# Turning x and h by DMA instead of on TensorE in an attention and fp4 feed-forward kernel, with u's statistics on ScalarE

## The chip, the cores and the metric

The kernel runs on one core of a Trainium2 chip. The metric is the device time of one execution in microseconds (us), the median of several runs. Engines: PE is TensorE (matmuls; PEld is its weight load), DVE is VectorE, ACT is ScalarE, POOL is GpSimd, SP is SyncE, which here only issues DMAs. Each engine runs its own instructions in the order of the program and waits on semaphores for the others.

## What is computed

32 batches of x and of a context, each 256 rows by 512 columns. First a grouped gating over the rows, then a feed-forward layer whose operands are rounded to fp4 in blocks of 16. Cut to what matters:

```python
q = layernorm(x)
t, p, g = Wt @ ctx, Wp @ q, Wg @ ctx            # 256x256 weights over the rows
att = sum over each group of 32 rows of p * g, * 0.125
u = Wz_group @ (att * t)                         # scaled later: Wz @ Wt is folded into one weight
xn = (u - mean_group(u)) / sqrt(var_group(u) + eps)
x1 = x + xn * gamma + beta + ctx
a = fp4_quant_dequant(layernorm(x1))             # blocks of 16: scale = max|.|/6, nearest of 8 magnitudes
h = silu(a @ fp4(w_gate).T) * (a @ fp4(w_up).T)  # 1408 hidden columns
out = x1 + fp4_quant_dequant(h) @ fp4(w_down).T
```

## The kernel before, in words

The rows are worked in **tiles** of 128: 32 batches (index i) of 2 tiles (s = 0, 1), 64 tiles in all, j = 2i + s. All weights stay on chip; the first 180 us or so round and split them. After that one body per batch runs (`body`, once for each engine), unrolled for the first and the last two batches and a hardware loop between.

The work of a tile is staged over several tiles. In tile j, PE does, in this order:

- `scores(j+2)` (L413): p, g and u of tile j+2, 18 matmuls of 512 columns. The p and g products go to PSUM bank `pairs`, u to `ubank`.
- `hidden(j, c)` for c = 0 to 3 (L449): gate and up products, 24 matmuls of 352 columns for each c. Every fp32 operand is a sum of two fp16 parts, hi and lo, so each product is three matmuls. The weights side of PE holds x's turned parts `xT`.
- between these groups `turn_h(j-1, r)` for r = 0 to 2 (L440): transposes of 4, 4 and 3 blocks of 128x128 of `hq`, the rounded h of tile j-1, into PSUM `tbank`; after c = 1 also `group_means(j+2)` (L421), after c = 2 also `group_spread(j+2)` (L426), two tiny matmuls each waiting for statistics of u.
- `output(j-1)` (L461): 33 matmuls of 512 columns into `obank`, from the turned h of tile j-1.
- `turn_x(j+1)` (L432): 4 transposes of the rounded x of tile j+1.

Behind each transpose of a set, ACT rounds the PSUM copy to fp16 (`split_hi`, L605), and DVE subtracts it to get the lo part (`split_lo`, L753).

DVE carries most of the elementwise work: the product sum of p and g (`sum_pg`, L777), statistics of u (`u_moments` L782, `u_mean` L786), the second layernorm (`residual` L805, `x1_moments` L809, `x1_mean` L813, `normalise2` L819), the rounding of x in 512-column instructions, the gate product (`gated`, L897) after each silu of ACT (L694), the rounding of h in 1408-column instructions (`h_first` L746, `h_scales`, `h_units`, `h_y` L725, `h_snap_add` L734, `h_snap_back` L738, `h_finish` L742), and the store's last step (`emit`, L906). The rounding to a grid of eight magnitudes needs one ACT step in its middle (`grain`, L620). POOL makes the small per-row columns (`columns`, `columns_affine`, L1137 to L1155), two inverse roots and the lo parts of context and q (`ctx_lo` L1123, `q_lo` L1129), and x + ctx (`add_ctx` L1118). SP loads x and context two batches ahead (L331, L337) and stores each tile (L356).

Within a tile the order on each engine is written out by hand in `body`. What binds the engines to one another: `hidden(j, c)` needs `gated(j, c-2)` (two pairs of PSUM banks), `hidden(j, 1)` needs `sum_pg(j+2)`, `output(j-1)` needs the turned parts of h, `hidden(j, 0)` those of x.

Of the kernel before, what the change touches and what calls it, by code (L numbers as in the profile page):

```python
# [17 lines left out]
P = 128  # L18
# [37 lines left out]
def build(nc, x, ctx_in, Wt, Wp, Wg, Wz, gamma, beta, w_gate, w_up, w_down, out):  # L56
# [18 lines left out]
    with ExitStack() as stack:  # L75
# [52 lines left out]
        u_st = sb("u_st", [P, 6])  # L128
# [15 lines left out]
        xT = [[sb(f"xT{s}_{part}", [P, KD, P], F16) for part in ("hi", "lo")] for s in range(2)]  # L144
# [14 lines left out]
        o_sb = early[:, 2 * GW:].rearrange("p (a b) -> p a b", a=2)  # L159

# [53 lines left out]
        u_stats = sem("u_stats")  # L214
# [111 lines left out]
        def _(sp):  # L326
# [47 lines left out]
            load_raw(5)  # L374

            def body(i):
                ahead = not isinstance(i, int) or i + 2 < NB
                for s in range(HT):
# [5 lines left out]
                    if not isinstance(j, int) or j > 0:  # L384
                        store(j - 1, 1 - s)
# [5 lines left out]
            body(NB - 1)  # L391
            store(NT - 1, 1)
# [5 lines left out]
        def _(pe):  # L398
# [29 lines left out]
            def turn_x(t, bank):  # L428

                pe.wait_ge(xq_ready, t + 1)  # L430
                for k in range(KD):
                    mm = pe.transpose(bank[:, k * P:(k + 1) * P], xq[:, k * P:(k + 1) * P], ident[:, :])  # L432
                mm.then_inc(x_turned, 1)

            def turn_h(j, r):

                pe.wait_ge(hq_ready, 3 * j + r + 1)
                k0, nk = SETS[r]
                for k in range(nk):
                    mm = pe.transpose(tbank[:, (r + 1) % 2, k, :], hq[:, (k0 + k) * P:(k0 + k + 1) * P], ident[:, :])  # L440
                mm.then_inc(h_turned, 1)

# [11 lines left out]
            def output(j):  # L454

                at_least(pe, o_ready, j)
                for r, (k0, nk) in enumerate(SETS):
                    pe.wait_ge(h_lo_done, 3 * j + r + 1)
                    for k in range(k0, k0 + nk):
                        for part, wpart in PARTS:  # L460
                            mm = pe.matmul(obank[:, :], hT[part][:, k, :], w2[wpart][:, k, :],  # L461
                                           start=(k == 0 and part == 0 and wpart == 0), stop=(k == KH - 1 and part == 1))
# [48 lines left out]
            for n in range(PHASES):  # L511
# [16 lines left out]
                if n == 8:  # L528
                    turn_x(0, obank)

            def body(i):
                more = not isinstance(i, int) or i + 1 < NB
                for s in range(HT):
# [7 lines left out]
                    pe.wait_ge(x_lo_done, j + 1)  # L541
                    if first:
                        pe.wait_ge(w_lo_done, FINAL[0][0])
                    for c in range(GROUPS):
# [9 lines left out]
                        if c > 0 and not first:  # L554

                            if c != 2:
                                at_least(pe, h_lo_done, 3 * (j - 1) + (c - 2 if c == 3 else 0))
                            turn_h(j - 1, c - 1)
                        if c == 1 and more:
                            group_means(j + 2)  # L560
                        if c == 2 and more:
                            group_spread(j + 2)
                    if not first:
                        output(j - 1)
                    if more or s == 0:

                        if first:
                            pe.wait_ge(w_lo_done, len(weight_sets))
                        at_least(pe, h_lo_done, 3 * (j - 1) + 2)
                        turn_x(j + 1, tbank[:, 0].rearrange("p k n -> p (k n)"))  # L570
# [6 lines left out]
            for r in range(3):  # L577
                pe.wait_ge(h_lo_done, 3 * (NT - 1) + max(r - 1, 0))
                turn_h(NT - 1, r)
# [4 lines left out]
        def _(act):  # L584
# [5 lines left out]
            def copy_u(t):  # L590
                act.wait_ge(u_done, t + 1)
                at_least(act, u_stats, t)
                at_least(act, v_ready, t)
                nc.scalar.copy(u_sb[:, :], ubank[:, :]).then_inc(u_copied, 1)
# [54 lines left out]
            for n in range(PHASES):  # L649
# [4 lines left out]
                if n in SCORES_OF:  # L654
                    copy_p(SCORES_OF[n], 0)
                    copy_u(SCORES_OF[n])
                sets = sets_of_phase(n)
# [9 lines left out]
                if n == 8:  # L667
                    act.wait_ge(x_turned, 1)
                    nc.scalar.copy(xT[0][0][:, :, :].rearrange("p k n -> p (k n)"), obank[:, :]).then_inc(x_hi_done, 1)
# [5 lines left out]
            def body(i):  # L675
                ahead = not isinstance(i, int) or i + 2 < NB
                more = not isinstance(i, int) or i + 1 < NB
                for s in range(HT):
                    j = HT * i + s
                    first = isinstance(j, int) and j == 0  # L680
                    if more and not first:
                        copy_p(j + 2, s)
                    if not first:
                        grain(hm[:, :], h[:, :], h_y_done, j, h_grain_done)
                    if more and not first:
                        copy_u(j + 2)
                    if ahead and s == 1:
                        ctx_hi(i + 2)
                    for c in range(GROUPS):
# [6 lines left out]
                        if first:  # L696
                            for one in final_sets(c):
                                weights_hi(one)
                        if c == 0 and ahead and s == 1:
                            q_hi(i + 2)  # L700
                        if c > 0 and not first:
                            k0, nk = SETS[c - 1]
                            split_hi(hT[0][:, k0:k0 + nk, :], c % 2, nk, h_turned, 3 * (j - 1) + c, h_hi_done)
                        if c == 2 and (more or s == 0):
# [559 lines left out]
```

## Time and profile before

| | us |
|---|---|
| median of 3 runs | 1982.62 (1979.66 to 1983.31) |
| the profiled execution's own time | 1983.16 |
| its span, first to last instruction | 1981.2 |
| PE busy | 1844.4 (93%) |
| DVE busy | 1610.4 (81%) |
| POOL busy | 737.0 (37%) |
| ACT busy | 620.4 (31%) |
| mean granted TensorE clock | 0.979 of full, 1.00 in the loop |

The profile is one execution. Busy time counts an engine's instructions, not its waits; matmuls overlap, so the durations of single matmuls add up to more than PE's busy time, and the time that one costs is the distance between two starts. DMA engines are busy 8% of the time in the steady part.

### The profile page before, as it was taken

Reading aid. Unit: us, or ns where it says so; the run is one execution under the profiler, and the core shown is the slowest. Engines: PE = TensorE matmul, PEld = TensorE weight load, DVE = VectorE, ACT = ScalarE, POOL = GpSimd, SP = SyncE. Lnnn points to the kernel's source line nnn. Section 1 sums busy time; section 2 is a strip of 40 time slices with the busy share of each in tenths; the row PEclk is TensorE's granted clock in tenths of the full one; section 3 lists DMA queues with packets and bytes.
Section 4 is the critical chain, followed back from the end, with each engine's and each line's share of the span. In section 5 each row is a group of like instructions: output and inputs, shape, how many; then the busy total and the mean of one; then the engine's idle time right before and its main releaser. Section 6 shows DMA issues by size and latency. Waiting matters only on the chain.

```text
span 1981.2 us, 32391 instructions
## 1 busy us (share of the span) xinstructions
PE 1844.4 (93%) x11022; PEld 1208.4 (61%) x11022; DVE 1610.4 (81%) x2885; ACT 620.4 (31%) x981; POOL 737.0 (37%) x1065
## 2 busy tenths in 40 slices
PE   2528899999999999999999999999999999999997
PEld 1427566666666666666666666666666666666664
DVE  5575888888888888888888888888888888888775
ACT  2324332333333332333233333333333333323221
POOL 4647443333333343433333343333333433333310
PEclk9769999999999999999999999999999999999999
DMA  5100010001000000000000000000010000100000
GB/s 183 51 0 22 17 33 16 32 32 32 16 32 32 32 25 23 32 32 32 16 32 32 32 21 26 32 32 32 16 32 32 32 16 32 32 32 27 11 11 17
DMA packets 32022, 60.11 MB, mean 30 GB/s; under 512 B 3072, under 2 KB 4352, under 8 KB 32000
## 3 DMA queue, kind: packets, MB, share of 16 engines
q1 hardware_dynamic: 32000, 59.81, 8.9%
q8 instruction: 14, 0.23, 0.0%
q14 instruction: 8, 0.07, 0.0%
HBM read 43.03 MB, written 16.78 MB: 30 GB/s over the span
## 4 chain that ended last, share of the span: by engine, by line
PE 41%; issue 20%; POOL 15%; DVE 12%; DMA 6%; ACT 4%; SPq 1%; DVEq 1%; POOLq 0%; ACTq 0%
PE pairs L449 19%; PE obank L461 12%; DMA c_in<-in_ctx 5%; POOL c_lo L1123 5%; PE pairs L413 5%; PE ubank L413 2%; ACT early L694 2%; DVE hT_parts L753 2%; ACT c_hi L610 2%; POOL q_lo L1129 1%; DVE ln_st L809 1%; DVE x L805 1%; DVE xT_lo L753 1%; POOL att L1151 1%; DVE early L906 1%
## 5 line engine op out<-in xcount | busy, mean ns | idle before, releaser
L461 PE MATMUL obank<-w_parts,hT_parts 128*128 128x512 f16 x2112 | 467.1, 380 | 0.0
L461 PEld LDWEIGHTS obank<-w_parts,hT_parts 128*128 128x128 f16 x2112 | 207.0, 98 | 235.4 <-issue 1.1
L449 PE MATMUL pairs<-w_gate_hi,xT_hi 128*128 128x352 f16 x1024 | 321.0, 313 | 7.8 <-DVE xT_lo L753 7.1
L449 PE MATMUL pairs<-w_gate_hi,xT_lo 128*128 128x352 f16 x1024 | 320.8, 313 | 0.0
L449 PE MATMUL pairs<-w_up_lo,xT_hi 128*128 128x352 f16 x1024 | 320.7, 313 | 0.0
L449 PE MATMUL pairs<-w_up_hi,xT_lo 128*128 128x352 f16 x1024 | 320.7, 313 | 0.0
L449 PE MATMUL pairs<-w_gate_lo,xT_hi 128*128 128x352 f16 x1024 | 320.7, 313 | 0.0
L449 PE MATMUL pairs<-w_up_hi,xT_hi 128*128 128x352 f16 x1024 | 320.5, 313 | 0.0
L897 DVE SCALAR_TENSOR_TENSOR h<-pairs,w_unit,early 128x352 f32<-128x352 f32 x256 | 149.5, 584 | 199.7 <-ACT early L694 195.6
L694 ACT ACTIVATE early<-pairs,w_unit 128x352 f32<-128x352 f32 x256 | 140.1, 547 | 366.3 <-PE pairs L449 366.3
L1123 POOL TENSOR_TENSOR c_lo<-c_in,c_hi 128x512 fp32r<-128x512 f32 x64 | 98.2, 1554 | 179.8 <-ACT c_hi L610 172.9
L1159 POOL TENSOR_TENSOR ln_rs<-ln_mv,eps_col 128x1 f32<-128x1 f32 x64 | 13.5, 211 | 382.3 <-DVE ln_mv L813 382.3
L449 PEld LDWEIGHTS pairs<-w_gate_hi,xT_hi 128*128 128x128 f16 x1024 | 110.6, 108 | 68.5 <-issue 17.5
L605 ACT CAST xT_hi<-tbank 128x512 f16<-128x512 f32 x63 | 36.8, 585 | 333.9 <-PE tbank L432 333.9
L742 DVE SCALAR_TENSOR_TENSOR hq<-h,h_unit 128x512 f32<-128x512 f32 (+1 forms) x192 | 139.5, 781 | 2.0
L1137 POOL TENSOR_TENSOR att<-rowst,grp 128x1 f32<-128x1 f32 x64 | 14.8, 230 | 329.7 <-DVE grp L791 329.7
L449 PEld LDWEIGHTS pairs<-w_up_hi,xT_lo 128*128 128x128 f16 x1024 | 100.4, 98 | 52.9
L449 PEld LDWEIGHTS pairs<-w_gate_hi,xT_lo 128*128 128x128 f16 x1024 | 100.3, 98 | 53.1
L449 PEld LDWEIGHTS pairs<-w_up_lo,xT_hi 128*128 128x128 f16 x1024 | 100.2, 98 | 53.1
L449 PEld LDWEIGHTS pairs<-w_gate_lo,xT_hi 128*128 128x128 f16 x1024 | 100.1, 98 | 53.0
L449 PEld LDWEIGHTS pairs<-w_up_hi,xT_hi 128*128 128x128 f16 x1024 | 100.3, 98 | 43.0
L753 DVE TENSOR_TENSOR hT_parts<-tbank,hT_parts 128x512 f16<-128x512 f32 (+1 forms) x192 | 122.1, 636 | 1.6 <-ACT hT_parts L605 1.6
(172 smaller groups left out, 3615.7 us busy)
## 6 DMA issues: line engine op xcount, KB each, us to landing
x_in<-in_x SPq DMA_DIRECT2D x32, 512.0 KB, 3.4
c_in<-in_ctx SPq DMA_DIRECT2D x32, 512.0 KB, 3.5
out<-early SPq DMA_DIRECT2D x64, 256.0 KB, 2.1
raw<-in_L_ffn_w_down SPq DMA_DIRECT2D x2, 1408.0 KB, 8.8
raw<-in_L_ffn_w_gate SPq DMA_DIRECT2D x2, 1280.0 KB, 8.3
w_parts<-in_L_ffn_w_up SPq DMA_DIRECT2D x2, 1280.0 KB, 9.2
raw<-in_L_ffn_w_gate SPq DMA_DIRECT2D x2, 128.0 KB, 8.4
early<-in_L_xattn_Wt SPq DMA_DIRECT2D x1, 256.0 KB, 9.8
```

Of the source, the lines that this page charges most:

```text
L413: mm = pe.matmul(dst, wT[wpart][:, k, s * P:(s + 1) * P], src[part][:, k, :], start=(k == 0 and wpart == 0 and part == 0), stop=(k == HT - ...
L449: mm = pe.matmul(pairs[:, pair, n, 0:GW], xT[s][part][:, k, :], w1[n][wpart][:, k, c * GW:(c + 1) * GW], start=(k == 0 and part == 0 and w ...
L461: mm = pe.matmul(obank[:, :], hT[part][:, k, :], w2[wpart][:, k, :], start=(k == 0 and part == 0 and wpart == 0), stop=(k == KH - 1 and pa ...
L605: nc.scalar.copy(dst, tbank[:, bank, 0:n, :]).then_inc(done, 1)
L610: nc.scalar.copy(c_parts[0][:, :, :], c_in[:, :, :]).then_inc(c_hi_done, 1)
L694: nc.scalar.activation(silu[:, c % 2, :], pairs[:, (s + 1 + c) % 2, 0, 0:GW], ACT.Silu, scale=w_unit[:, 0:1]).then_inc(silu_done, 1)
L742: nc.vector.scalar_tensor_tensor(out=blocks(q_out), in0=blocks(y), scalar=-factor, in1=over_block(scale), op0=ALU.mult, op1=ALU.mult).then ...
L753: nc.vector.tensor_tensor(dst, tbank[:, bank, 0:n, :], hi, ALU.subtract).then_inc(done, 1)
L805: nc.vector.tensor_tensor(x1[:, t % 4, :], v_sb[:, :], xc[:, s, :], ALU.add).then_inc(x1_ready, 1)
L809: nc.vector.bn_stats(ln2_st[:, :], x1[:, t % 4, :]).then_inc(ln2_stats, 1)
L897: nc.vector.scalar_tensor_tensor(out=h[:, c * GW:(c + 1) * GW], in0=pairs[:, (s + 1 + c) % 2, 1, 0:GW], scalar=w_unit[:, 1:2], in1=silu[:, ...
L1123: nc.gpsimd.tensor_tensor(c_parts[1][:, s, :], c_in[:, s, :], c_parts[0][:, s, :].bitcast(F32), ALU.subtract).then_inc(c_ready, 1)
```

## The change

- **Turning by DMA.** `turn_x` and `turn_h` are taken off PE. ACT and DVE now make the hi and lo parts of the untransposed x and h in SBUF (`x_hi`, `h_hi` on ACT, `x_lo`, `h_lo` on DVE; h in two pieces of 704 columns), side by side in a free stretch of `raw`, and SP issues one transposing DMA for each tile's x (8 blocks of 128x128 fp16) and one for its h (22 blocks). PE waits for the DMA's semaphore.
- **u's statistics on ScalarE.** ACT sums u while it copies it, makes minus the mean, squares the deviations with a sum, and makes the variance (`u_moments` on ACT, four instructions with the copy). DVE's two instructions go. The mean has the other sign, so one POOL subtraction is an addition.
- **Order within a tile.** DVE: both snap steps of h stand ahead of `sum_pg`; the whole first half of x's rounding comes between the first and the second gate product, `x_finish` after the second, `x_lo` after the third; the residual and its statistics come after h's first half. ACT: h's `grain` is at the tile's end, x's `grain` after the second silu, `affine` after the fourth. PE: `group_spread` after c = 3. POOL: `q_lo` after `columns`.

```diff
-            def turn_x(t, bank):          # on PE
-            def turn_h(j, r):             # on PE
...
+            def turn_x(t, s):             # on SP
+                made = t + 1 if isinstance(t, int) else sp.to_reg(t + 1)
+                wait_apart(sp, minus_made, x_lo_done, made)
+                sp.dma_start_transpose(xT_parts[s][:].rearrange("p a k n -> p (a k) n"),
+                                       xq_parts.rearrange("p a k -> p (a k)")).then_inc(x_turned, 16)
+            def turn_h(j):                # on SP
+                made = 2 * j + 2 if isinstance(j, int) else sp.to_reg(2 * j + 2)
+                wait_apart(sp, minus_made, h_lo_done, made)
+                sp.dma_start_transpose(hT_parts[:].rearrange("p a k n -> p (a k) n"),
+                                       hq_parts.rearrange("p a k -> p (a k)")).then_inc(h_turned, 16)
...
             def output(j):
                 at_least(pe, o_ready, j)
-                for r, (k0, nk) in enumerate(SETS):
-                    pe.wait_ge(h_lo_done, 3 * j + r + 1)
-                    for k in range(k0, k0 + nk):
+                pe.wait_ge(h_turned, 16 * j + 16)
+                for k in range(KH):
...
+            def u_moments(t):             # on ACT
+                at_least(act, grp_done, t)
+                at_least(act, sq_steps, 2 * t)
+                act.wait_ge(u_copied, t + 1)
+                nc.scalar.activation(rowst[:, 1:2], u_sum[:, 0:1], ACT.Identity, scale=-1.0 / D).then_inc(u_mean_made, 1)
+                act.wait_ge(u_mean_made, t + 1)
+                nc.scalar.activation(u_dev[:, :], u_sb[:, :], ACT.Square, bias=rowst[:, 1:2],
+                                     accum_out=u_sum[:, 1:2]).then_inc(u_squared, 1)
+                act.wait_ge(u_squared, t + 1)
+                nc.scalar.activation(rowst[:, 2:3], u_sum[:, 1:2], ACT.Identity, scale=1.0 / D).then_inc(rowst_ready, 1)
+            def x_hi(t):
+                act.wait_ge(xq_ready, t + 1)
+                at_least(act, x_turned, 16 * t)
+                nc.scalar.copy(xq_parts[:, 0, :], xq[:, :]).then_inc(x_hi_done, 1)
+            def h_hi(j):
+                at_least(act, h_turned, 16 * j)
+                for r, (a, b) in enumerate(HPIECES):
+                    act.wait_ge(hq_ready, 2 * j + r + 1)
+                    nc.scalar.copy(hq_parts[:, 0, a:b], hq[:, a:b]).then_inc(h_hi_done, 1)
...
-            def u_moments(t):             # on DVE: bn_stats
-            def u_mean(t):                # on DVE: bn_aggr
...
+            def h_lo(j):
+                for r, (a, b) in enumerate(HPIECES):
+                    dve.wait_ge(h_hi_done, 2 * j + r + 1)
+                    nc.vector.tensor_tensor(hq_parts[:, 1, a:b], hq[:, a:b], hq_parts[:, 0, a:b],
+                                            ALU.subtract).then_inc(h_lo_done, 1)
+            def x_lo(t):
+                dve.wait_ge(x_hi_done, t + 1)
+                nc.vector.tensor_tensor(xq_parts[:, 1, :], xq[:, :], xq_parts[:, 0, :],
+                                        ALU.subtract).then_inc(x_lo_done, 1)
```

How the instructions stand now, at three places.

**PE, in the loop's first tile, from the end of hidden group c = 1 (L449; L463 in the change) to the start of c = 2.** `tbank<-ident,hq` are h's transposes. Before:

```order
L449 MATMUL pairs<-w_gate_hi,xT_lo 128x352
L449 MATMUL pairs<-w_up_hi,xT_lo 128x352
L45 REGISTER_ALU
L437 REGISTER_ALU
L440 MATMUL tbank<-ident,hq 128x128 x4
L421 MATMUL ubank<-rowst,gmean 128x3
L45 REGISTER_ALU
L449 MATMUL pairs<-w_gate_hi,xT_hi 128x352
```

Of the change:

```order
L463 MATMUL pairs<-w_gate_hi,xT_parts 128x352
L463 MATMUL pairs<-w_up_hi,xT_parts 128x352
L450 MATMUL ubank<-rowst,gmean 128x3
L45 REGISTER_ALU
L463 MATMUL pairs<-w_gate_hi,xT_parts 128x352
```

The four transposes are gone from between the groups, and so are those after c = 2 and c = 3 and the four of x after `output`.

**DVE, in the loop, from the store's last step of one tile to the first gate product (`h<-pairs,w_unit,early`) of the next.** Before:

```order
L906 SCALAR_TENSOR_TENSOR early<-obank,o_unit,x 128x512
L45 REGISTER_ALU
L775 REGISTER_ALU
L777 SCALAR_TENSOR_TENSOR p_sb,rowst<-pairs,p_sb 128x512
L734 SCALAR_TENSOR_TENSOR h<-hm,h 128x1408
L782 BN_STATS u_st<-u_sb 128x6
L738 SCALAR_TENSOR_TENSOR h<-hm,h 128x1408
L786 BN_AGGR rowst<-u_st 128x2
L742 SCALAR_TENSOR_TENSOR hq<-h,h_unit 128x512 x2
L742 SCALAR_TENSOR_TENSOR hq<-h,h_unit 128x384
```

Of the change (`raw<-hq,raw` is `h_lo`):

```order
L925 SCALAR_TENSOR_TENSOR early<-obank,o_unit,x 128x512
L751 SCALAR_TENSOR_TENSOR h<-hm,h 128x1408
L755 SCALAR_TENSOR_TENSOR h<-hm,h 128x1408
L45 REGISTER_ALU
L792 REGISTER_ALU
L794 SCALAR_TENSOR_TENSOR p_sb,rowst<-pairs,p_sb 128x512
L759 SCALAR_TENSOR_TENSOR hq<-h,h_unit 128x704 x2
L900 REGISTER_ALU
L901 TENSOR_TENSOR raw<-hq,raw 128x704
L900 REGISTER_ALU
L901 TENSOR_TENSOR raw<-hq,raw 128x704
```

The two statistics are gone, the product sum stands behind both snap steps, and the lo parts of h are made here, ahead of the first gate product.

**SP, one batch of the loop.** Before:

```order
L331 DMA x_in<-in_x 128x2x512
L355 REGISTER_ALU
L356 ISA
L356 DMA out<-early 128x512
L337 DMA c_in<-in_ctx 128x2x512
L355 REGISTER_ALU
L356 ISA
L356 DMA out<-early 128x512
```

Of the change:

```order
L339 DMA x_in<-in_x 128x2x512
L371 ISA
L373 DMA_TRANSPOSE hT_parts<-raw 128x22x128
L364 REGISTER_ALU
L366 DMA_TRANSPOSE xT_parts<-raw 128x8x128
L378 ISA
L378 DMA out<-early 128x512
L345 DMA c_in<-in_ctx 128x2x512
L371 ISA
L373 DMA_TRANSPOSE hT_parts<-raw 128x22x128
L364 REGISTER_ALU
L366 DMA_TRANSPOSE xT_parts<-raw 128x8x128
```

Two transposing DMAs stand in each tile ahead of the store; each waits on SP for its lo parts, and what stands behind it waits too.

## Rows read from the trace of the kernel before

**Rows 1.** The page: busy us, share of the span and instructions of each engine.

```profile
PE 1844.4 (93%) x11022; PEld 1208.4 (61%) x11022; DVE 1610.4 (81%) x2885; ACT 620.4 (31%) x981; POOL 737.0 (37%) x1065
```

**Rows 2.** One batch of the loop: us; PE, PEld, DVE, ACT, POOL busy; PEclk; DMA.

```profile
897.74:953.65 55.91, 55.42 (x334) 35.85 (x332) 47.34 (x89) 17.68 (x28) 20.38 (x33) 1.00 0.08 28
```

**Rows 3.** Timeline of PE over one tile: start, us, instruction, count, idle before.

```profile
905.06 0.47 PE L413 MATMUL pairs<-q_hi,wpT_hi 128*128 128x512 f32 x1
...
909.34 0.32 PE L449 MATMUL pairs<-w_gate_hi,xT_hi 128*128 128x352 f16 x1
...
916.51 0.60 PE L440 MATMUL tbank<-ident,hq 128*128 128x128 f32 x4
916.95 0.28 PE L421 MATMUL ubank<-rowst,gmean 128*128 128x3 f32 x2
917.09 0.31 PE L449 MATMUL pairs<-w_gate_hi,xT_hi 128*128 128x352 f16 x1
...
924.83 0.49 PE L440 MATMUL tbank<-ident,hq 128*128 128x128 f32 x3
925.15 7.29 PE L461 MATMUL obank<-w_parts,hT_parts 128*128 128x512 f16 x33
932.27 0.60 PE L432 MATMUL tbank<-ident,xq 128*128 128x128 f32 x4
932.63 0.48 PE L413 MATMUL pairs<-q_hi,wpT_hi 128*128 128x512 f32 x1
```

**Rows 4.** Who waited for whom, 300 to 1900 us: total us, times, longest.

```profile
PEld ubank L426 <- POOL att L1140: 19.7, 28, 0.7
```

**Rows 5.** Groups by line and shape, 300 to 1900 us: busy us, mean ns.

```profile
L897 DVE SCALAR_TENSOR_TENSOR h<-pairs,w_unit,early 128x352 f32<-128x352 f32 x231 | 134.9, 584 | 168.6 <-ACT early L694 164.8
...
L734 DVE SCALAR_TENSOR_TENSOR h<-hm,h 128x1408 f32<-128x1408 bf16 x57 | 92.4, 1620 | 0.0
...
L753 DVE TENSOR_TENSOR hT_parts<-tbank,hT_parts 128x512 f16<-128x512 f32 x116 | 78.9, 680 | 0.0
...
L620 ACT ACTIVATE hm<-h 128x1408 bf16<-128x1408 f32 x57 | 78.8, 1382 | 0.0
...
L742 DVE SCALAR_TENSOR_TENSOR hq<-h,h_unit 128x512 f32<-128x512 f32 x114 | 73.7, 688 | 1.8
...
L742 DVE SCALAR_TENSOR_TENSOR hq<-h,h_unit 128x384 f32<-128x384 f32 x57 | 57.2, 1003 | 0.0
...
L782 DVE BATCH_NORM_STATS2 u_st<-u_sb 128x6 f32<-128x512 f32 x57 | 39.1, 687 | 0.0
...
L786 DVE BATCH_NORM_AGGREGATE rowst<-u_st 128x2 f32<-128x6 f32 x57 | 9.9, 175 | 0.0
```

**Rows 6.** The page's costliest groups: ACT's silu (us, mean ns, idle before).

```profile
L694 ACT ACTIVATE early<-pairs,w_unit 128x352 f32<-128x352 f32 x256 | 140.1, 547 | 366.3 <-PE pairs L449 366.3
```

**Rows 7.** DMA issues: KB each, median us from issue to landing.

```profile
x_in<-in_x SPq DMA_DIRECT2D x32, 512.0 KB, 3.4
...
out<-early SPq DMA_DIRECT2D x64, 256.0 KB, 2.1
raw<-in_L_ffn_w_down SPq DMA_DIRECT2D x2, 1408.0 KB, 8.8
```

**Rows 8.** Groups by line and shape: POOL's one-column steps, behind and before the spread.

```profile
L1151 POOL TENSOR_TENSOR att<-att 128x1 f32<-128x1 f32 x57 | 38.4, 674 | 4.5
...
L1142 POOL TENSOR_TENSOR att<-att 128x1 f32<-128x1 f32 x58 | 11.2, 193 | 0.0
```

**Rows 9.** Timeline of the last tile's end, DVE and PE.

```profile
1955.97 1.61 DVE L746 TENSOR_REDUCE h_amax<-h 128x88 f32<-128x1408 f32 x1
...
1959.20 1.62 DVE L725 SCALAR_TENSOR_TENSOR h<-h,h_rinv 128x1408 f32<-128x1408 f32 x1
...
1965.84 1.76 DVE L742 SCALAR_TENSOR_TENSOR hq<-h,h_unit 128x512 f32<-128x512 f32 x3
...
1969.86 8.12 PE L461 MATMUL obank<-w_parts,hT_parts 128*128 128x512 f16 x33
```

More of the change, by code:

```diff
@@ L143, in build @@
         x_rinv = sb("x_rinv", [P, XB])
-        xT = [[sb(f"xT{s}_{part}", [P, KD, P], F16) for part in ("hi", "lo")] for s in range(2)]
+        xT_parts = [sb(f"xT_parts{s}", [P, 2, KD, P], F16) for s in range(2)]
+        xT = [[xT_parts[s][:, part] for part in range(2)] for s in range(2)]
         silu = early[:, 0:2 * GW].rearrange("p (a b) -> p a b", a=2)
@@ L374, in _ @@
             load_raw(5)
+            turn_x(0, 0)
             def body(i):
                 ahead = not isinstance(i, int) or i + 2 < NB
+                more = not isinstance(i, int) or i + 1 < NB
                 for s in range(HT):
@@ L384, in body @@
                     if not isinstance(j, int) or j > 0:
+                        turn_h(j - 1)
+                    if more or s == 0:
+                        turn_x(j + 1, 1 - s)
+                    if not isinstance(j, int) or j > 0:
                         store(j - 1, 1 - s)
@@ L456, in output @@
                 at_least(pe, o_ready, j)
[L457 to L462 removed]
+                pe.wait_ge(h_turned, 16 * j + 16)
+                for k in range(KH):
+                    for part, wpart in PARTS:
+                        mm = pe.matmul(obank[:, :], hT[part][:, k, :], w2[wpart][:, k, :],
+                                       start=(k == 0 and part == 0 and wpart == 0), stop=(k == KH - 1 and part == 1))
                 mm.then_inc(o_done, 1)
@@ L553, in body @@
                                 turn_weights(one)
[L554 to L558, printed above, removed]
                         if c == 1 and more:
                             group_means(j + 2)
-                        if c == 2 and more:
+                        if c == 3 and more:
                             group_spread(j + 2)
                     if not first:
+                        if isinstance(j, int) and j == 1:
+                            pe.wait_ge(w_lo_done, len(weight_sets))
                         output(j - 1)
[L565 to L570, printed above, removed]
             body(0)
@@ L682, in body @@
                         copy_p(j + 2, s)
+                        copy_u(j + 2)
                     if not first:
[L684 to L688, printed above, removed]
+                        h_hi(j - 1)
                     for c in range(GROUPS):
@@ L715, in _ @@
             body(NB - 1)
-            grain(hm[:, :], h[:, :], h_y_done, NT, h_grain_done)
-            for r, (k0, nk) in enumerate(SETS):
-                split_hi(hT[0][:, k0:k0 + nk, :], (r + 1) % 2, nk, h_turned, 3 * (NT - 1) + r + 1, h_hi_done)
+            h_hi(NT - 1)
         @block.vector
@@ L1015, in body @@
                     quant_x = more or s == 0
+                    if not first:
+                        h_snap_add(j - 1)
+                        h_snap_back(j - 1)
                     if more:
@@ L1227, in body @@
                         ctx_lo(i + 2)
+                    columns(t, s)
+                    if ahead and s == 1:
                         q_lo(i + 2)
-                    columns(t, s)
                     columns_affine(t, s)
```

124 lines of the change are left out of this document (45 added, 79 removed).

## Prediction

> **What bounds the kernel now.** I read the page first: PE is busy 93% of the span, DVE 81%, the others about a third [rows 1]. Then the busy time of one batch, two tiles of the loop: 55.91 us, of which PE is busy 55.42, at the full granted clock of 1.00 [rows 2]. So a tile takes 27.95 us and PE hardly rests. DVE is busy 47.34 us of the two tiles, 23.7 us a tile: second, but 4 us behind. Then PE's timeline over one tile [rows 3], by distances between starts: scores 905.06 to 909.34, 4.28 us; two hidden groups 909.34 to 916.51, 3.58 each; four h transposes 0.44 (916.51 to 916.95); the mean matmuls 0.14 (to 917.09); the last three h transposes 0.32 (924.83 to 925.15); output 7.12 (to 932.27); four x transposes 0.36 (to 932.63). PE's own work is the bound, so what leaves PE's queue leaves the time, as long as nothing else comes late.
>
> **The change, part by part.**
>
> *PE's transposes.* A tile loses two sets of 0.44 and one each of 0.32 and 0.36: 1.56 us. There are 63 such tiles in the loops (h of tiles 0 to 62, x of tiles 1 to 63): -98.3 us.
>
> *The wait in front of the spread matmuls.* In every second tile PE's weight load waits for POOL's column, 0.70 us each (19.7 over 28 [rows 4]), because POOL first does the lo parts of context and q. The change puts the spread behind group 3, 3.58 us later, and `q_lo` behind the column. The wait should vanish in the 30 batches that load ahead: -21 us. What is late next there: `variance`, POOL's columns, ACT's `affine` and DVE's residual all move by a group; below I find them in time.
>
> A tile then takes PE 4.28 + 4 x 3.58 + 2 x 0.14 + 7.12 = 26.0 us.
>
> *DVE.* The rows give 1.62 us for 1408 columns and 0.68 for 512, so 1.05 ns a column: 0.88 for 704, 0.55 for 384 [rows 5]. Gone: the two statistics, 0.69 + 0.18 [rows 5]; three lo splits of h from PSUM, 0.68 + 0.68 + 0.55; three `hq` instructions of 0.69, 0.69 and 1.00 [rows 5]. New: two `hq` and two lo instructions of 704 columns. The sum is 23.7 - 0.87 - 1.91 - 2.38 + 4 x 0.88 = 22.0 us, 85% of 26.0. DVE's share rises, its slack stays 4 us a tile.
>
> *ACT.* The hi casts move from PSUM to SBUF, two of 704 columns by ACT's rows (1.38 us for 1408, 0.55 for 352 [rows 5, 6], so 0.79 ns a column) 0.82 each; u's square and sum over 512 columns is about 0.7, at most 0.2 more for each of its sum and its two one-column steps. ACT is busy under 9 us a tile [rows 2]; 1.5 more cost nothing by themselves. Their order matters: u's three steps stand behind the first silu and are needed by the mean matmuls 7.2 us after hidden starts, about 2 us later than they are ready.
>
> *The chain that now decides*, in us from a tile's first scores matmul. DVE: `emit` ends at 1.1, two snap steps of 1.6 [rows 5] to 4.3, `sum_pg` 5.0, two `hq` 6.7, and the lo parts, the second behind ACT's second hi cast, 8.4. There the h turn may start. PE reaches output at 4.28 + 14.32 + 0.28 = 18.9. So **the h turn has 10.5 us**, from its semaphore on SP to landing. The x turn: third gate product (silu and gate 0.55 + 0.58 behind the group [rows 5, 6]) at 16.4, `x_lo` 17.1, needed at 26.0 + 4.3 = 30.3, so 13 us. At the end of the tile: last gate product 20.1, h's maximum and scales 3.2 (1955.97 to 1959.20 [rows 9]) to 23.3, `h_y` 24.9, residual and two statistics 1.6 more, 26.5, ACT's `grain` 26.3. It closes with DVE about 0.4 us behind the end of output, so that `emit` ends at 1.1 of the next tile, and PE does not wait for that: `sum_pg` at 5.0 is needed by group 1 at 7.9, the first gate product at 9.1 by group 2 at 11.6. Sums like these are good to about 0.5 us, and the smallest slack outside the h turn is over 2 us.
>
> *The transposing DMA.* No row of before shows one. An h turn moves 128 x 2816 fp16, 704 KB. From below: a plain load of 512 KB lands in 3.4 us [rows 7]; by its rate 704 KB take 4.7. From above: 22 blocks one behind the other, each at the time of the smallest plain DMA of a tile, 2.1 us [rows 7], 46 us. These ends are far apart. I take 7 us, one and a half times the plain copy, since the row it is nearest to in bytes and in form (one instruction, 128 partitions, 16 engines) is a load, and the 1408 KB row (8.8 us) says that such DMAs grow by their bytes, not by a fixed price for each piece. Any value under 10.5 gives the same time. Above it a tile is 8.4 + L + 7.1 = 15.5 + L, with L the h turn. Break-even with 27.95 is **L = 12.4 us**. The Trainium skill (DMA: Bandwidth & Descriptors, Latency and other measured facts) gives 261 GB/s for a transposing DMA with a strided middle dimension; by that estimate L is 2.8 us and PE's 26.0 stand. No run here has shown it yet.
>
> *SP.* A turn is 0.4 us of issue by today's DMAs and each waits in SP's order. Behind h's stand x's turn and the store; x's semaphore comes 9 us after h's, the store is not waited for until its buffer is used two tiles later, and the loads of x and context (3.4 us) are needed a tile later. Nothing.
>
> *The first 180 us.* DVE loses three pairs of statistics, ACT gains three sets of about 1.4 us in the midst of the weights. I take +1 us, between -3 and +4. The first x turn has over 20 us of room.
>
> *The end.* Before, `hq` starts at 1965.84 and output 4.0 us later and takes 8.12 us where it takes 7.12 in the loop [rows 9, 3]. Now 1.8 for `hq`, 0.8 for the hi cast of the second piece, 0.9 for the lo, and the whole turn of 7: output 10.5 us after `hq`, 6.5 later than now. PE has then been idle for 14 us instead of 5, and the output already loses 1.0 us to a lower clock today; I add 1.5. Together +8, between +4 and +12.
>
> *Sum:* against the profiled execution's 1983.2 (0.6 above the median of the runs, which is nothing): 1983.2 - 98.3 - 21 + 1 + 8 = **1873 us**.
>
> **The rivals.**
>
> *A: the turn pays by the block, and the kernel gets slower.* If each 128x128 block of the 22 costs 0.9 us of its own (under half of the smallest DMA's 2.1), L is 20 us, a tile 35.5, and the time 1873 + 63 x 9.5 = about 2470. It decides from L = 12.4, 0.56 us a block. For it: that a DMA with 256-byte rows and a turn inside has no row in this profile. Against: today's DMAs keep the engines busy 8% of the time and cost by bytes. The Trainium skill speaks for it (VectorE: DVE Perf Modes, The three transpose paths): 1309 ns for a 128x128 transpose by DMA. If blocks did not overlap, its estimate is 22 x 1.31 = 29 us for h alone, a tile of 44.5 and about 3040 us in all; I give that reading less weight than the page on DMAs, since one block alone pays the fixed part that 22 share. Chance 0.17.
>
> *B: something on DVE, ACT or POOL comes late.* POOL's one-column instructions take 0.67 us beside DVE's rounding and 0.19 beside light work [rows 8], and the third `hq`, the smallest, takes 1.00 us where 0.55 is its size [rows 5]: DVE and POOL hold each other up where both read SBUF. The lo parts of h and x now read two SBUF operands, where one was PSUM. DVE has 4 us to spare in sum but waits at eight places in a fixed order. Each 0.5 us that a tile gets longer is 32 us: 1905 at +0.5, 1936 at +1. An h turn of 11 to 12 us would end in the same place. Chance 0.13.
>
> *C: the turns leave PE but the time stays*, because a new wait of 1.6 to 2 us a tile takes their place. That needs L within 0.2 us of 12.4, or DVE at 27.9. Chance 0.02.
>
> **The numbers.** My forecast, PE bound at 26.0 a tile, has a chance of 0.68: 1873, by itself between 1858 (the small terms at their low ends and PE's other short waits gone) and 1895. A 0.17, B 0.13, C 0.02. A difference of 0.2%, 4 us, is about what a measurement of this kernel can tell. Faster: 0.68 + 0.13 = 0.81; same 0.02; slower 0.17. The range reaches from 1855 over B's cases to 1960; it leaves out A, C and little of the rest.
>
> **What would show it.** In the changed profile: no transposes on PE in the loop; a batch in 52.0 us with PE busy over 98%; PE's idle time before the first output matmul near zero; the h turn landing 4 to 10 us after issue; DVE at 85% with its idle time split between the four silus; no wait at the spread. Wrong if PE waits at the output for the DMA (A), then the batch is 2 x (15.5 + L); or if PE waits at group 1 to 3 for gate products or for u's mean (B). The end should show one idle stretch of PE of 13 to 15 us before the last output; if it is under 8, L is smaller than I took.

## The result, and the profile after

The change makes the kernel faster: 1893.24 us, median of four runs (1892.27 to 1894.71), against 1982.14 for the kernel before (1979.66 to 1983.31). The ratio is 0.9554, 95% interval 0.9537 to 0.957. The profiled execution took 1893.97 us, its span 1892.2. The forecast was 1873, the gain 89 us where 110 was expected. The bound stayed where it was put, on PE; the steady tile is 0.5 us longer than the forecast's 26.0, and 0.6 us longer than PE's own work as later runs show it (25.93, e9).

The page's first part, which answers to [rows 1]:

```profile
PE 1742.4 (92%) x10062; PEld 1098.9 (58%) x10062; DVE 1656.3 (88%) x2629; ACT 719.6 (38%) x1237; POOL 805.8 (43%) x1065
```

960 matmuls are gone, DVE has 256 instructions fewer and yet 46 us more of busy time. One batch, columns as in [rows 2]:

```profile
946.22:999.30 53.08, 52.32 (x304) 32.48 (x303) 48.85 (x82) 20.82 (x36) 22.93 (x32) 1.00 0.29 67
```

PE rests 0.76 us of 53.08 where nothing was to be left of 52.0, and DVE is busy 48.85 us in 82 instructions, more than the 47.34 in 89 of before. So DVE's instructions have become longer, which the sum had not allowed for. The list of who waited for whom, 300 to 1800 us, PE and its weight load (us in total, times, longest):

```profile
PE ubank L450 <- ACT rowst L603: 12.2, 28, 0.4
PE pairs L463 <- DVE h L916: 9.1, 28, 0.3
...
PEld pairs L463 <- DVE h L916: 19.1, 28, 0.7
```

The wait at the spread [rows 4] is gone. Two others have come, each in one tile of every batch: the mean matmuls wait for ACT's statistics (even tile), and the last hidden group for the second gate product (odd tile). PE waits for no DMA in the loop. DVE in the even tile, whose scores start at 919.77 (start, us, line, count), the rows in front of its first gate product:

```profile
922.43 1.62 DVE L751 SCALAR_TENSOR_TENSOR h<-hm,h 128x1408 f32<-128x1408 bf16 x1
924.08 2.58 DVE L755 SCALAR_TENSOR_TENSOR h<-hm,h 128x1408 f32<-128x1408 bf16 x1
...
927.20 2.15 DVE L759 SCALAR_TENSOR_TENSOR hq<-h,h_unit 128x704 f32<-128x704 f32 x2
929.39 1.70 DVE L901 TENSOR_TENSOR raw<-hq,raw 128x704 f16<-128x704 f32 x2
931.00 0.58 DVE L916 SCALAR_TENSOR_TENSOR h<-pairs,w_unit,early 128x352 f32<-128x352 f32 x1
```

The second snap step takes 2.58 us where the first, of the same size, takes 1.62. POOL's and SP's rows of the same tile:

```profile
922.47 5.32 POOL L1117 TENSOR_TENSOR xc<-x_in,c_in 128x512 f32<-128x512 f32 x2
```

```profile
931.16 3.34 SPq L373 DMA_TRANSPOSE hT_parts<-raw  x1
939.41 1.23 SPq L366 DMA_TRANSPOSE xT_parts<-raw  x1
```

POOL's addition of the context, `add_ctx`, lies right beside the snap step and `hq`. The h turn is issued 11.4 us into the tile, not 8.4. The page's DMA issues (median us from issue to landing), the rows that no profile of before had:

```profile
xT_parts<-raw SPq DMA_TRANSPOSE x64, 3.1
hT_parts<-raw SPq DMA_TRANSPOSE x64, 5.2
```

The end, to set beside [rows 9]:

```profile
1879.67 9.18 PE L474 MATMUL obank<-w_parts,hT_parts 128*128 128x512 f16 x33 [12.88 <-DMA hT_parts<-raw]
```

**Where the 89 us between the two profiles come from**, by the starts of the 64 output stages. The first is 3.6 us earlier (223.57 for 227.17). The next 59 steps take 26.43 and 26.60 us in turn, mean 26.52, where they took 27.93: -83.5. Three steps of the last batches bring -8.0. The last step costs +4.8 and the last output 9.18 us for 8.12, +1.1. Together -89.

### The profile page after: what moved, and what is told of

The parts are those of the page before. It is cut to its first block, busy times and chain, and to the rows that moved or that the text cites. A ratio compares the mean times of both kernels' runs of the same rounds, so it can differ in the third digit from the quotient of the medians.

```text
span 1892.2 us, 30546 instructions
## 1 busy us (share of the span) xinstructions
PE 1742.4 (92%) x10062; PEld 1098.9 (58%) x10062; DVE 1656.3 (88%) x2629; ACT 719.6 (38%) x1237; POOL 805.8 (43%) x1065
## 4 chain that ended last, share of the span: by engine, by line
PE 40%; DVE 35%; issue 16%; ACT 5%; POOL 2%; DVEq 1%; DMA 1%; ACTq 0%; SPq 0%; POOLq 0%
PE pairs L463 19%; PE obank L474 13%; PE pairs L442 4%; DVE hq L759 3%; DVE q L785 3%; DVE h L751 3%; DVE h L916 3%; DVE h L742 3%; ACT early L711 3%; DVE h_amax L763 3%; PE ubank L442 2%; DVE x L814 1%; ACT u_dev L600 1%; DVE ln_st L818 1%; DVE xn L755 1%
## 5 line engine op out<-in xcount | busy, mean ns | idle before, releaser
L463 PE MATMUL pairs<-w_gate_hi,xT_parts 128*128 128x352 f16 x2048 | 629.3, 313 | 16.1 <-DVE h L916 11.7
L463 PE MATMUL pairs<-w_up_hi,xT_parts 128*128 128x352 f16 x2048 | 628.4, 313 | 0.0
L474 PE MATMUL obank<-w_parts,hT_parts 128*128 128x512 f16 x2112 | 468.0, 380 | 12.9 <-DMA hT_parts<-raw 12.9
L463 PE MATMUL pairs<-w_up_lo,xT_parts 128*128 128x352 f16 x1024 | 320.4, 313 | 0.0
L463 PE MATMUL pairs<-w_gate_lo,xT_parts 128*128 128x352 f16 x1024 | 320.3, 313 | 0.0
L463 PEld LDWEIGHTS pairs<-w_gate_hi,xT_parts 128*128 128x128 f16 x2048 | 205.3, 100 | 142.5 <-DVE h L916 23.3
L463 PEld LDWEIGHTS pairs<-w_up_hi,xT_parts 128*128 128x128 f16 x2048 | 200.6, 98 | 97.5
L1117 POOL TENSOR_TENSOR xc<-x_in,c_in 128x512 f32<-128x512 f32 x64 | 166.0, 2614 | 0.0
L755 DVE SCALAR_TENSOR_TENSOR h<-hm,h 128x1408 f32<-128x1408 bf16 x66 | 138.2, 2094 | 2.2
L463 PEld LDWEIGHTS pairs<-w_up_lo,xT_parts 128*128 128x128 f16 x1024 | 100.2, 98 | 52.8
L463 PEld LDWEIGHTS pairs<-w_gate_lo,xT_parts 128*128 128x128 f16 x1024 | 100.2, 98 | 52.8
L759 DVE SCALAR_TENSOR_TENSOR hq<-h,h_unit 128x704 f32<-128x704 f32 x128 | 121.9, 992 | 0.1
L901 DVE TENSOR_TENSOR raw<-hq,raw 128x704 f16<-128x704 f32 x128 | 108.5, 890 | 3.0
```

Of the source, the lines that this page charges most:

```text
L463: mm = pe.matmul(pairs[:, pair, n, 0:GW], xT[s][part][:, k, :], w1[n][wpart][:, k, c * GW:(c + 1) * GW], start=(k == 0 and part == 0 and w ...
L755: nc.vector.scalar_tensor_tensor(out=y, in0=m, scalar=GRAIN, in1=y, op0=ALU.max, op1=ALU.subtract).then_inc(done, 1)
L759: nc.vector.scalar_tensor_tensor(out=blocks(q_out), in0=blocks(y), scalar=-factor, in1=over_block(scale), op0=ALU.mult, op1=ALU.mult).then ...
L901: nc.vector.tensor_tensor(hq_parts[:, 1, a:b], hq[:, a:b], hq_parts[:, 0, a:b], ALU.subtract).then_inc(h_lo_done, 1)
L1117: nc.gpsimd.tensor_tensor(xc[:, s, :], x_in[:, s, :], c_in[:, s, :], ALU.add).then_inc(xc_ready, 1)
```

## The experiments

Three theories for the half microsecond that each tile takes too long. **T** (POOL): `add_ctx` and DVE's steps hold each other up, and so the lo parts and all behind them are late. **Q** (order): the steps stand in a queue in which something else comes first: ACT's statistics of u behind h's casts, q's layernorm ahead of the second gate product. **D**: the turns' DMA traffic slows DVE.

**1. e1: `add_ctx` over 8 of 512 columns.** From the third batch on x + ctx is made in 8 columns only, so that part of the output is left out.

```diff
-                    nc.gpsimd.tensor_tensor(xc[:, s, :], x_in[:, s, :], c_in[:, s, :], ALU.add)...
+                    nc.gpsimd.tensor_tensor(xc[:, s, 0:n], x_in[:, s, 0:n], c_in[:, s, 0:n], ALU.add)...
```

> GpSimd's sum of x and context (add_ctx) is made over 8 of 512 columns from the third batch on, so that part of the output is left out. Theory T (VectorE and GpSimd hold each other up when both read SBUF, and what comes late of it makes PE wait): the second snap step of the even tile falls from 2.58 us to 1.62, the wait of the mean matmuls for ACT's statistics goes, a batch falls from 53.04 us to 52.4 to 52.6, and the time to about 1876. Rival Q (only the order of the queues makes the waits): batch 53.04 within 0.1, time 1893. Rival D (the transposing DMAs slow VectorE's SBUF reads): the snap step stays at 2.58 us and the batch at 53.0.

Measured: 1860.66 us, one run beside 1981.5 of before. The batch, and the group of h's second snap step (busy us, mean ns):

```profile
905.99:957.83 51.84, 51.84 (x303) 32.48 (x302) 47.61 (x81) 20.96 (x36) 19.40 (x32) 1.00 0.30 68
```

```profile
L755 DVE SCALAR_TENSOR_TENSOR h<-hm,h 128x1408 f32<-128x1408 bf16 x58 | 95.4, 1644 | 2.0
```

PE is now busy all of the batch: 25.92 us is a tile of its own work, and both new waits are gone. The snap step falls from a mean of 2094 ns to 1644 with the DMAs unchanged (share 0.30), so D falls. T is right in kind and was sized too small, 1876 for 1861: without this one overlap the whole 33 us are gone.

**2. e2: `ctx_lo` and `q_lo` over 8 columns too.** These parts of context and q are left out as well.

```diff
-                        ctx_lo(i + 2)
+                        ctx_lo(i + 2, 8)
...
-                        q_lo(i + 2)
+                        q_lo(i + 2, 8)
```

> As the run before, and the lo parts of context and q over 8 of 512 columns too, from the third batch on. Theory T: all of VectorE's lengthened instructions (the first snap product of x 1.31 us, q 1.94 for two, x's lo part 1.62 in the odd tile) fall to 0.68, 1.0 and 0.68, PE waits nowhere in the loop, a batch takes 52.0 us and the whole 1861. Rival Q: the odd tile still waits for its gate product, because q is normalised ahead of it, batch 52.7. Rival D: lengthened instructions stay, batch 53.0.

Measured: 1857.74 us, one run. DVE's busy time in 1500 us falls from 1374.7 (e1) to 1303.9, since in the odd tile x's lo part and q's halves are back at 0.68 and 0.5 us each. That buys 2.9 us between two single runs, and 2.5 of them lie ahead of the first output stage (224.31 to 221.76): in this loop DVE, behind the bound, may work 70 us longer and cost next to nothing. Only the overlap ahead of a step that PE waits for has a price. Rival Q's 52.7 for the batch is out: a step is 25.93 us.

**3. e3: the same length of addition, u's statistics first.** The addition is whole again; ACT makes u's statistics right behind the copy of u, ahead of h's casts.

```diff
                         copy_u(j + 2)
+                        u_moments(j + 2)
...
-                        if c == 0 and more and not first:
-                            u_moments(j + 2)
```

> ACT makes u's three statistics steps right behind the copy of u, ahead of h's hi casts, instead of behind the first silu. Rival Q: the mean matmuls' wait for ACT (0.44 us and 0.2 around it in the even tile) goes wholly, 0.65 us a batch, time 1873. Theory T: the wait goes too, but the first gate product of the even tile ends (931.58) only as PE would start the third group (931.57), so 0.1 to 0.3 us come back: 0.4 to 0.55 a batch, time 1877 to 1881.

Measured: 1871.04 us (1870.85 to 1871.13), ratio to before 0.9441, interval 0.9425 to 0.9456. That is a little under Q's 1873, and outside T's 1877 to 1881. The wait at the means is gone. In the changed kernel ACT stands idle for 3.5 us in front of `h_hi` in the even tile, the very stretch into which u's statistics fit. Left is the odd tile's (same columns as above):

```profile
PEld pairs L463 <- DVE h L915: 12.3, 28, 0.5
```

**4. e4: and q's layernorm one gate product later.**

```diff
-                        if c == 0 and ahead and s == 1:
-                            normalise1(i + 2)
...
+                        if c == 1 and ahead and s == 1:
+                            normalise1(i + 2)
```

> The run before, and VectorE normalises q behind the second gate product and the group copy instead of ahead of the gate product. Both theories: the odd tile's wait for that gate product (0.33 us and what surrounds it) goes, 0.35 to 0.45 us a batch, 12 us in all on top of the run before: 1861 to 1869. With T the delay by GpSimd moves to x_finish, which has 1.2 us of room before the third gate product. If neither holds and the wait moves to the spread or the third group, the time equals that of the run before.

Measured: 1864.44 us (1863.22 to 1864.64), ratio 0.9406, interval 0.939 to 0.9422. As expected, 1861 to 1869. PE is busy 1498.84 of 1500 us. So both readings of the loss hold: with `add_ctx` short the order does no harm (e1), and with the order mended `add_ctx` does hardly any (e4). The loss takes both.

**5 and 6. e5, e6: each h turned twice, and three times.** PE waits for the last turn, the others write to a free stretch; the diff is of e5, e6 has 2 in place of 1.

```diff
+                for n in range(1):
+                    sp.dma_start_transpose(spare[n], hq_parts...).then_inc(again_turned[n], 16)
```

> Every h is turned twice, the first time into spare memory, and PE waits for the second. The turn's issue takes 3.34 us of SP and the landing 1.9 more, so L goes from 5.2 to 8.6 us. The prediction's room (10.5 us behind the lo parts at 8.4 of the tile) says: no change, batch 53.04, time 1893. By the trace of the change the lo parts end at 9.8 and 11.4 of the tile and leave 9.7 and 8.3 us: then the even tile is 0.3 us late, batch 53.1 to 53.5, time 1893 to 1907.

> Three turns of each h, PE waits for the last: L is 11.9 us if a turn's price is SP's issue of 3.34 us and 1.9 of landing. The prediction's formula (a tile is 15.5 + L) gives 27.4 us, a batch of 54.8 and about 1950. With the lo parts as late as the trace of the change has them (9.8 and 11.4), the batch is up to 59 us and the time up to 2080; a slower PE gives VectorE time to catch up, so I expect 56 to 58 and 1985 to 2050. If the three turns overlap (issue hidden behind the transfer), L is 8 or less and nothing changes.

Measured: e5 1901.55 us, e6 2110.82, one run each. Who waited for whom, 300 to 1800 us, e5 and then e6; then an output stage of e6, and a window over it:

```profile
PE obank L480 <- DMA hT_parts<-raw: 9.5, 29, 1.0
```

```profile
PE obank L480 <- DMA hT_parts<-raw: 126.8, 50, 3.6
```

```profile
909.55 8.98 PE L480 MATMUL obank<-w_parts,hT_parts 128*128 128x512 f16 x33 [3.56 <-DMA hT_parts<-raw]
```

```profile
909.50:918.60 9.10, 9.05 (x34) 3.95 (x35) 4.27 (x11) 2.04 (x2) 1.60 (x4) 0.81 0.08 14
```

SP issues the two turns of e5 in 3.40 and 3.45 us one behind the other and the last lands 1.8 later: L is 8.7 us. PE just begins to wait for the turn, 0.3 us in one tile of two. The room is therefore about 8.3 us in the even tile, as the rows of the changed kernel give (lo parts ready 11.3 us into it, output at 19.7), and not 10.5. In the loop that wait costs nothing: a batch takes 53.1 us as in the changed kernel, and the waits for the second gate product shrink instead (the weight load's from 19.1 us to 6.5). The 8 us by which e5 is longer lie outside the steady loop: the first output stage comes 1.5 us earlier, the second 2 later, the last batches lose about 3, and the end 4, where nothing hides the second turn.

With three turns L is 12.2 us and the time 2111, above the 1985 to 2050 that were expected, and far above what the prediction's formula 15.5 + L gives with L = 12: 63 x 1.5 us over the forecast, 1968. A tile takes 29.7 us in the mean. Two things that the formula lacks explain it. The lo parts come at 8.5 us in the odd tile and at 10.2 in the even one, beside `add_ctx`, and not at 8.4. And behind the longer wait, which comes in every even tile, the granted clock falls: the stage shown has 0.81 in the mean, a part of it at 0.50, the lower of the two levels (1.2 GHz), and takes 8.98 us where 7.28 is the row of a stage at 1.00. Over the whole loop the stages behind waits of 2.7 us and more take 8.6 to 10.2 us at 0.85 to 0.71, and those behind waits of 1.6 to 1.9 us all take 7.3 at 1.00.

**7. e7: the kernel before, with the spread and what hangs on it one group later** (variance and affine too; POOL's columns stand ahead of `q_lo`).

```diff
-                        if c == 2 and more:
+                        if c == 3 and more:
                             group_spread(j + 2)
```

> The kernel before with one part of the new order alone: the spread matmuls, the variance and affine one group later, and GpSimd's columns ahead of q's lo part. The prediction's term: 0.70 us a batch, 21 us in all, 1961. Rival: the residual that comes later on VectorE (behind affine) moves h's first half and the x turn, and the gain is half or less, 1970 to 1982.

Measured: 1989.67 us (1988.44 to 1990.29), ratio 1.0035, interval 1.0022 to 1.0047: the move gains nothing and costs 7 us, where 1961, or 1970 to 1982, was expected. The wait at the spread [rows 4] is gone from the list all the same. Its trace, DVE's residual and the wait of PE that has come instead:

```profile
905.93 0.69 DVE L805 TENSOR_TENSOR x<-v_sb,xc 128x512 f32 x1 [2.59 <-ACT v_sb L600]
```

```profile
PE pairs L449 <- DVE xT_lo L753: 12.9, 27, 0.6
```

DVE stands 2.6 us in front of the residual for ACT's `affine`, and x's lo parts, behind it, come late. In the changed kernel the residual stands behind h's first half: `affine` ends at 944.13 and the residual starts at 946.26, so there the later spread holds up nothing.

**8. e8: the kernel before, with u's statistics on ScalarE alone.**

```diff
-                nc.scalar.copy(u_sb[:, :], ubank[:, :]).then_inc(u_copied, 1)
+                nc.scalar.activation(u_sb[:, :], ubank[:, :], ACT.Identity, accum_out=u_sum[:, 0:1]).then_inc(u_copied, 1)
...
+                    u_moments(SCORES_OF[n])        # ACT
...
-                        u_moments(t)               # DVE
...
-                        u_mean(t)                  # DVE
```

> The kernel before with u's statistics on ScalarE alone. The prediction priced it at nothing for PE: VectorE loses 0.87 us a tile where it has 4 to spare. Expected 1982 within 4 us. If VectorE or GpSimd set a hidden wait (the odd tile's spread), it may come 0.3 to 0.7 us a batch earlier, 1960 to 1973.

Measured: 1963.08 us (1962.03 to 1966.62), ratio 0.9907, interval 0.989 to 0.9923. The wait of [rows 4] shrinks from 19.7 us over 28 to

```profile
PEld ubank L428 <- POOL att L1140: 2.6, 8, 0.6
```

The whole gain is 19.6 us, in the second of the two ranges. The first output stage starts 4.0 us earlier than before, and the 59 alike steps bring 14.7 us. The way there can be read from the odd tile, which starts at 932.63 in the kernel before and at 922.39 in e8. Before:

```profile
943.57 1.33 DVE L768 TENSOR_SCALAR q<-x_in,ln_mv,ln_rs 128x512 f32<-128x512 f32 x2
...
946.06 2.49 POOL L1129 TENSOR_TENSOR q_lo<-q,q_hi 128x512 fp32r<-128x512 f32 x2 [1.90 <-ACT q_hi L615]
```

In e8:

```profile
931.77 2.29 DVE L782 TENSOR_SCALAR q<-x_in,ln_mv,ln_rs 128x512 f32<-128x512 f32 x2
...
935.22 2.50 POOL L1129 TENSOR_TENSOR q_lo<-q,q_hi 128x512 fp32r<-128x512 f32 x2 [1.44 <-ACT q_hi L627]
```

With two instructions fewer, DVE starts q 9.4 us into the tile and not 10.9. Beside `c_lo` it takes longer, but it is still done 0.6 us earlier, and so are `q_lo` and the column behind it for which the spread waits. Earlier statistics are not the reason: the mean matmuls that read them start 11.9 us into the tile in both kernels and wait in neither. So this part takes away the wait for which the prediction had already counted 21 us, by another way.

**9. e9: e4, and `add_ctx` in two halves**, the first in the odd tile behind `columns_affine`, the second where it was.

```diff
                     columns_affine(t, s)
+                    if ahead and s == 1:
+                        add_ctx(i + 2, 0)
...
-                        add_ctx(i + 2)
+                        add_ctx(i + 2, 1)
```

> Nothing is left out of the computation. On top of e4, POOL's addition of the context is taken in two halves: the first half of a block right behind columns_affine in the odd tile, the second where it was. If the addition's length in one piece beside the even tile's snaps and lo parts is all that is left over the time of TensorE's own work (e4 runs 26.09 us a tile against 25.92 in e1, where the addition is nearly gone), then a part of at most 0.17 x 62 = 10 us is to be had: 1858 to 1862. If the half that is moved only meets other DVE work with two SBUF inputs (h_y, the residual), nothing is gained: 1863 to 1866, and in the odd tile h_y (1.62 us) reads over 2 us. If the odd tile has no room for it on POOL, the affine steps of the next tile come late and it loses: over 1868.

Measured: 1860.02 us (1858.6 to 1860.95), ratio 0.9383, interval 0.9367 to 0.9399. As expected, 1858 to 1862. Every steady step is 25.93 or 25.94 us. The two halves on POOL:

```profile
901.51 1.27 POOL L1116 TENSOR_TENSOR xc<-x_in,c_in 128x512 f32<-128x512 f32 x1
...
907.08 2.74 POOL L1116 TENSOR_TENSOR xc<-x_in,c_in 128x512 f32<-128x512 f32 x1
```

The moved half takes 1.27 us, and h's division (1.62 us, two operands in SBUF) starts only when it has ended, so the rival's "over 2 us" for it did not come. The other half still meets the snap steps. The first of them starts at 907.05, 0.03 us ahead of the addition, and keeps its 1.62 us; the addition takes 2.74 us for 1.27, and the second snap step, which starts in its midst at 908.70, 2.60 for 1.62. But there is now time for it. This version beats both kernels: 33 us under the changed one, with nothing left out.

**10. e10: the changed kernel with x's rounding at its old places.**

```diff
-                            x_first(j + 1)         # behind gate 1
-                            x_scales(j + 1)
-                            x_y(j + 1)
...
-                            x_finish(j + 1)        # behind gate 2
+                            x_first(j + 1)         # behind gate 2
+                            x_scales(j + 1)
...
+                            x_y(j + 1)             # behind gate 3
...
+                            x_finish(j + 1)        # ahead of gate 4
...
-                            x_lo(j + 1)            # behind gate 3
...
+                        x_lo(j + 1)                # behind h_y
```

> Nothing is left out of the computation. The changed kernel with x's rounding at the places it has in the kernel before (maximum and scales behind gate 2, division behind gate 3, q behind gate 4's place of before, lo part behind h's division), all else as changed. Room in the changed kernel's even tile: x's turn is issued 19.6 us into the tile, lands 3.1 later, and the xT parts are read 30.9 us in: 8 us of room. Behind h's division the lo part ends about 27.0 in, the turn lands at 30.1 to 31: about no room left, and the residual comes 0.7 us later. Theory T (the rounding's new place is what the turn by DMA needs, a room that is just used up): 0 to 1 us a tile more, 1895 to 1950, with waits of TensorE for the DMA of xT_parts in the list. Rival (the rounding between the gates is what delays the first and second gates, and so the wait of 19.1 us for h): without it gates come earlier, those waits vanish: 1875 to 1890, and no wait for xT_parts. Rival N: the two cancel, 1890 to 1896.

Measured: 1912.59 us (1912.13 to 1913.81), 19 us slower than the changed kernel. The waits, and PE's row at the start of the second tile:

```profile
PE ubank L450 <- ACT rowst L603: 23.6, 28, 0.8
PE pairs L463 <- DVE p_sb L794: 5.5, 28, 0.2
...
PEld pairs L463 <- DMA xT_parts<-raw: 0.3, 1, 0.3
```

```profile
210.95 0.47 PE L463 MATMUL pairs<-w_gate_hi,xT_parts 128*128 128x352 f16 x1 [6.77 <-DMA xT_parts<-raw]
```

By the starts of output: 3.7 us at the first (223.57 to 227.22), 10 in the 59 alike steps (25.98 and 27.38 for 26.43 and 26.60), 6 in two short steps of the last batches (26.72 and 24.73 for 22.99 and 22.50). In the steady loop the x turn still arrives in time; what is lost there is on DVE: the wait for the second gate product is gone, but the one at the means doubles and one for `sum_pg` is new. T's size was right and its mechanism seen at the start only; the rival's gain did not come. So the rounding of x between the gates, taken out of the changed kernel, is worth about 19 us of the 89.

## Why the prediction came out as it did

- **What bounds the kernel**: right. PE is busy 98.6% of the batch, and in e1, e4 and e9 over 99.9% of 1500 us. Its own tile is 25.92 us in e1, where the sum had 26.0.
- **PE's transposes, -98.3**: right. In e9 a tile costs 25.93 against 27.93, 2.0 us, of which 1.56 was this term and about 0.4 the spread's wait and smaller ones. No run turns by DMA and changes nothing else, so the term is shown by what is left, not by itself.
- **The wait at the spread, -21**: the wait is gone as forecast, and its size was right. The cause that was named, the move of the spread, does take it away (e7), but in the old order x's lo parts then come late and the kernel loses 7 us. The step that failed stands beside it: u's statistics on ACT were priced at nothing for PE. e8 makes that change alone and gains 19.6 us, mostly by the same wait, since DVE comes to q earlier. The changed kernel has both; no run takes only one of them out of it, so which of them it needs stays open.
- **DVE 22.0 us a tile, 85%**: wrong, and the step that cost the time. It is 24.4 us (48.85 a batch), 92% and not 85%; with all of POOL's large steps short (e2) it is 22.5, near the sum. The durations were taken from rows of the old order, where `add_ctx` lay beside other work. In the new order it meets h's second snap step, 2.58 us for 1.62, and `hq`, 2.15 for 1.69; in the odd tile q's halves take 1.94 us for 1.0 beside `c_lo`, x's lo part 1.62 for 0.68 beside `q_lo`. Rival B named this very mechanism and its price for 0.5 us a tile, 1905; the tile came out at 26.52, 0.52 over the forecast of 26.0. A third of that was given back at the start, in the last tiles and at the end, by terms that the sum had otherwise; that the time lies between forecast and rival is in this part luck.
- **"Their order matters: u's three steps ... about 2 us later than they are ready"**: wrong, though a reserve was named. The 7.2 us in front of the mean matmuls were used up: the first silu came at 930.07, behind the late casts, u's last step ended at 931.78, and PE waited 0.44 us. e3 puts the steps where ACT is idle and gains 22 us.
- **The chain to the h turn, 8.4 us**: 11.3 in the even tile, 9.8 in the odd. The room is 8.3 us in the even tile, not 10.5; e5, with L at 8.7, waits 0.3 us there.
- **The turn, 7 us**: 5.2, nearer to the plain copy's rate (4.7) than I took it; under either value nothing depends on it. The Trainium skill's 261 GB/s (DMA: Bandwidth & Descriptors, Latency and other measured facts) gave 2.8 us: the measured 704 KB in 5.2 us are 139 GB/s. Over SP's issue alone, 3.34 us, they are 216 GB/s; the 1.8 us of landing, which the smaller turn has too, are the larger part of the difference. The Trainium skill's 1309 ns for one 128x128 block (VectorE: DVE Perf Modes, The three transpose paths) must not be multiplied: 22 blocks take 3.34 us of issue, 0.15 each.
- **Break-even at L = 12.4**: wrong. e6 with L at 12.2 takes 2111 us, slower than before by 6%. By the changed kernel's 9.8 and 11.3, mean 10.5, the same formula gives 27.93 = 10.5 + L + 7.1, so L of about 10.3; by e6's 8.5 and 10.2 it would be 11.4, less what the lower clock costs. These are estimates: no run lies between 8.7 and 12.2.
- **SP, nothing**: right for PE's time, with a wrong price behind it. The issue of an h turn takes 3.34 us and that of an x turn 1.23, where 0.4 was taken from the plain DMAs; but PE waits for nothing that stands behind them on SP.
- **The start, +1**: -3.6 by the first output stage, only -0.3 by the first hidden matmul (182.24 to 181.90). e8 has -4.0 at the first output stage without any turn by DMA, so the gain fits u's statistics; profiles of different runs differ there by some us, and this was not tested further. **The end, +8**: +5.9, since the turn is 5.2 us and not 7. PE's idle stretch is 12.9 us, under the 13 to 15 named, for the same reason.

The sum of the misses: +30 in the 59 alike tiles; -5 at the start; -3 in the three short steps of the last batches, against the 5.4 us that the tile terms leave for them; -2 at the end. That is 20 or 21 in all, for the 21 us between 1873 and the profiled 1893.97.

## What to carry to other kernels

Where DVE and POOL both read SBUF side by side, an instruction's duration belongs to its neighbour as much as to itself (1.62 or 2.58 us for the same snap step): when an order is laid out anew, ask of each long instruction of one engine what will now stand beside it on the other, and give the part that is waited for the stretch where the other is idle. Of a large change each part is best measured on both sides, added to the kernel before (e7, e8) and taken from the kernel after (e3, e10); the part that was counted as free can be the one that pays. An engine with slack in sum may still hold up the bound by one instruction in the wrong place.

## What the runs showed that I had not expected

- A DVE step with two SBUF operands beside POOL's: 1.62 us becomes 2.58 (128x1408), and POOL's addition takes 5.32 us where two halves of 1.27 are possible. DVE's q, with one tensor operand, is held up too: 0.53 us a half alone, 0.97 beside `c_lo`.
- SP needs 0.15 us of issue for each 128x128 block of a turn (3.34 us for 22, 1.23 for 8), the landing follows 1.8 us later, and two turns one behind the other add their issue alone.
- With three turns the waits of 2.7 us and more in front of the output bring the granted clock of the stage behind them to 0.71 to 0.85, where behind waits of 1.6 to 1.9 us it stays at 1.00, as it does in the whole loop of e5. In this kernel a late transfer is so paid for more than once.
